# Low parts of h on VectorE with four buffers, the down product four units behind, stores on GpSimd's queue

## What is computed

```python
x = x + tanh(g_xattn[0]) * xattn(layernorm(x), ctx, Wq, bq, Wk, bk, Wv, bv, Wo, bo)   # 16 heads of 8
x = x + tanh(g_ffn[0])   * ffn(layernorm(x), ...)

# ffn, on x of (1792 tokens, 128)
logits  = x @ router_w.T + expert_bias                   # 160 experts
top_w, top_idx = top_k(sigmoid(logits), 8)
top_w   = top_w / (sum(top_w) + 1e-9) * 2.5
combine = zeros(T, 160); combine[t, top_idx] = top_w
h1w     = silu(einsum('th,eih->eti', x, w_gate)) * combine.T[:, :, None]     # 64 wide
routed  = einsum('eti,ehi->th', h1w, w_down)
shared  = silu(x @ w_gate_shared.T) @ w_down_shared.T
```

## Time and profile before

| | us |
|---|---|
| median of 3 runs | 1157.08 |
| lowest, highest | 1156.97, 1157.84 |
| the profiled execution | 1156.67 |
| its span, first to last instruction | 1155.1 |
| mean granted TensorE clock, as a share of full speed | 0.979 |

### The profile page before, as it was taken

The page is one execution under the profiler, slowest core; times in us unless marked ns, Lnnn a source line. Parts: engine busy times, 40 slices in busy tenths (PEclk is TensorE's granted clock), DMA queues, the critical chain, the costliest instruction groups (busy, mean ns, idle before and its releaser), DMA issues.

```text
span 1155.1 us, 37333 instructions
## 1 busy us (share of the span) xinstructions
PE 1072.5 (93%) x12102; PEld 708.9 (61%) x12102; DVE 965.2 (84%) x1695; ACT 845.5 (73%) x1810; POOL 613.2 (53%) x991
## 2 busy tenths in 40 slices
PE   3699899999999999999999998875999999999998
PEld 1376677777777777777777776522455555555554
DVE  4778688888888888888888888464999999999998
ACT  3476677777777777777777776544788888888887
POOL 6796987887888788788788884343000000000000
PEclk9899999999999999999999999978999999999999
DMA  7876867576675775767657523342588878877784
GB/s 158 158 177 164 171 171 170 129 195 154 150 182 134 177 168 147 173 146 176 169 131 192 126 79 77 116 129 74 200 224 239 231 228 229 234 228 239 223 231 124
DMA packets 229436, 197.10 MB, mean 171 GB/s; under 512 B 160687, under 2 KB 207343, under 8 KB 229398
## 3 DMA queue, kind: packets, MB, share of 16 engines
q1 hardware_dynamic: 218468, 174.14, 59.2%
q0 software_dynamic: 8960, 20.99, 6.4%
q10 hardware_dynamic: 1970, 1.49, 0.6%
HBM read 109.96 MB, written 12.55 MB: 106 GB/s over the span
## 4 chain that ended last, share of the span: by engine, by line
PE 73%; DVE 11%; issue 5%; SPq 4%; POOL 3%; DMA 3%; ACT 1%; DVEq 0%; POOLq 0%
PE bank L1500 15%; PE bank L1490 15%; PE bank L1301 11%; PE bank L1334 10%; PE bank L1315 10%; DVE part_max L968 6%; PE bank L1370 4%; PE bank L1358 4%; DVE rec L1106 3%; POOL ctT L672 1%; PE bank L1413 1%; SPq L412 1%; SPq L367 1%; DMA ctx_in<-in_ctx_dram 1%; SPq L359 1%
## 5 line engine op out<-in xcount | busy, mean ns | idle before, releaser
L761 ACT ACTIVATE p_exp<-bank 125x448 f32<-125x448 f32 x768 | 400.4, 544 | 193.1 <-PE bank L1315 192.0
L968 DVE TENSOR_REDUCE part_max<-bank 128x1 f32<-128x500 f32 x672 | 420.4, 670 | 70.0 <-PE bank L1334 69.2
L1315 PE MATMUL bank<-q_st,k_stk 97*125 97x224 f16 x1536 | 274.9, 263 | 10.0 <-DMA q_st<-neg_row 6.6
L1334 PE MATMUL bank<-kparts,q_blk 128*128 128x500 f16 x672 | 255.1, 383 | 15.8 <-DVE part_max L968 13.1
L1315 PEld LDWEIGHTS bank<-q_st,k_stk 97*125 97x125 f16 x1536 | 197.2, 138 | 74.2 <-ACT p_exp L761 12.7
L825 ACT ACTIVATE ctT<-bank 128x448 f32<-128x448 f32 x320 | 173.9, 544 | 57.0 <-PE bank L1490 24.0
L1500 PE MATMUL bank<-ctT,w_ring 128*128 128x448 f16 x864 | 210.6, 352 | 0.1
L831 ACT ACTIVATE ctT<-xnT 128x448 f16<-128x448 f32 x320 | 182.1, 569 | 20.2 <-DVE xnT L1157 17.7
L1301 PE MATMUL bank<-p_exp,v_sb 125*25 125x168 f32 (+1 forms) x6144 | 186.7, 262 | 2.3 <-DVE o_raw L982 2.3
L1166 DVE TENSOR_TENSOR ctT<-xnT,ctT 128x448 f16<-128x448 f32 (+1 forms) x297 | 183.7, 619 | 0.1
L1301 PEld LDWEIGHTS bank<-p_exp,v_sb 125*25 125x25 f32 x6144 | 142.5, 104 | 44.6 <-issue 2.5
(11 more groups left out here) (178 smaller groups left out, 1371.9 us busy)
## 6 DMA issues: line engine op xcount, KB each, us to landing
k_stk<-kparts SPq DMA_DIRECT2D x384, 93.8 KB, 3.3
v_sb<-c_scratch SPq DMA_DIRECT2D x72, 448.0 KB, 4.3
k_stk<-c_scratch SPq DMA_DIRECT2D x72, 448.0 KB, 4.3
ctx_in<-in_ctx_dram SPq DMA_DIRECT2D x30, 672.0 KB
w_scratch<-w_out POOLq DMA_DIRECT2D x80, 128.0 KB, 3.1
w_in<-in_L_ffn_w_gate_dram POOLq DMA_DIRECT2D x80, 64.0 KB, 3.3
w_in<-in_L_ffn_w_down_dram POOLq DMA_DIRECT2D x80, 64.0 KB, 3.4
ctx_in<-in_ctx_dram SPq DMA_DIRECT2D x30, 78.0 KB
```

Of the source, the lines that this page charges most:

```text
L761: act.activation(p_exp[0:KP, j % PR, f * 448:(f + 1) * 448], ST[f][0:KP, 0:448], ACT.Exp).then_inc(exp_done, 1)
L968: v.reduce_max(part_max[:, i // NCH, i % NCH:i % NCH + 1], SM[i % NSM][:, 0:CK], axis=AX.X).then_inc(sm_maxed, 1)
L1315: last = pe.matmul(ST[f][0:KP, (g % 2) * GC:(g % 2 + 1) * GC], k_stk[0:97, u, g, j * KP:(j + 1) * KP], q_st[0:97, u, g, :, :].rearrange("p ...
L1334: pe.matmul(SM[i % NSM][:, 0:CK], rows, kparts[:, u, 0, c * CK:(c + 1) * CK], start=True, stop=True).then_inc(sm_done, 1)
```

## The change

- The ahead stage's low parts move from POOL to DVE: `lo_part(k-1)` is issued behind `weigh(k)`; those of units 0 to 2 stand ahead of unit 3. POOL's loop L667 to L672 is gone.
- h has four places in this stage too. `h_f` moves from `xnT` to a part of `v_sb`. PE does down of unit k-4 ahead of up of unit k; only downs 0 and 1 stand ahead of unit 6.
- The four stores of combine weights are issued by POOL, behind its last `comb` operation; SP only waits for `c_stored[t]`.
- `c_first[t]` becomes two semaphores, one for each pair of DMAs, and DVE waits for the half that it reads next. The last tile is loaded by eight DMAs, two for each two experts, with one semaphore for each two.
- `late_scale` (four scalings) moves from DVE to ACT, as do the copy of the last tile's tokens into `xnT` and the two copies of its combine weights (`last_weights`). DVE gets one small operation, `late_shift`.
- `sums` goes ahead of `replaced` and has three instructions instead of four.
- Slots: the top 8 of tiles 1 and 2 one slot and one slot later, the transposes of the combine weights three slots earlier; in the ahead stage late rows after unit 3 (was 5), tokens at 10 (12), logits at 13 (15), sigmoid at 17 (18), top 8 at 18 (19), last transposes at 25 (24).

```diff
-    TOP_AT = {(B + 1, 1): 0, (B + 1, 2): 1, (B + 1, 3): 2}
-    COMBT_AT = {(B + 1, 8): 0, (B + 1, 11): 1, (B + 2, 2): 2}
+    TOP_AT = {(B + 1, 1): 0, (B + 1, 3): 1, (B + 1, 4): 2}
+    COMBT_AT = {(B + 1, 5): 0, (B + 1, 8): 1, (B + 1, 11): 2}
-    OUT_LATE, TOKENS_LATE, LOGITS_LATE, COMBT_LATE = 5, 12, 15, 24
+    ROWS_LATE, SCALE_LATE, TOKENS_LATE, LOGITS_LATE, PROB_LATE, TOP_LATE, COMBT_LATE = 3, 8, 10, 13, 17, 18, 25
...
-        h_f = xnT[:, :].rearrange("p (a t) -> p a t", a=NTC)
+        h_f = v_words[:, 2 * N:3 * N].rearrange("p (a t) -> p a t", a=NTC)
...
             for t in range(TS):
-                store(t)
+                sp.wait_ge(c_stored[t], 16)
                 for j in range(2):
                     for a in range(2):
...
-                        sp.dma_start(c_pairs[j][a::2, t, :, :], src).then_inc(c_first[t], 16)
+                        sp.dma_start(c_pairs[j][a::2, t, :, :], src).then_inc(c_first[t][j], 16)
...
-            store(TS)
+            sp.wait_ge(c_stored[TS], 16)
             sp.wait_ge(pv_done, B * KT)
-            for a in range(2):
-                src = c_scratch[0:AHEAD, a, TS * TC:N].unsqueeze(0).to_broadcast([I, AHEAD, TC])
-                sp.dma_start(c_last[a::2, :, :], src).then_inc(c_late, 16)
+            for j in range(AHEAD // 2):
+                for a in range(2):
+                    src = c_scratch[2 * j:2 * j + 2, a, TS * TC:N].unsqueeze(0).to_broadcast([I, 2, TC])
+                    sp.dma_start(c_last[a::2, 2 * j:2 * j + 2, :], src).then_inc(c_late[j], 16)
...
-            for k in range(TAIL):
-                b = k % TS
-                rows = slice(0, I if k < TS else 128)
-                pool.wait_ge(hh_done, k + 1)
-                until(pool, dn_done, earlier(k))
-                pool.tensor_tensor(h_lo[rows, b, :], h_f[rows, b, :], h_hi[rows, b, :], ALU.subtract).then_inc(hl_done, 1)
+            for c in range(NTC):
+                pool.wait_ge(cb_cp, 2 * c + 2)
+                pool.dma_start(c_scratch[:, :, c * TC:(c + 1) * TC], combT[0:EP, :, c * TC:(c + 1) * TC]).then_inc(c_stored[c], 16)
...
+            def late_scale():
+                act.wait_ge(shift_made, 1)
+                for p in range(*LATE):
+                    i = p - LATE[0]
+                    last = act.activation(xc[:, p, :], xt[:, p, :], ACT.Identity, scale=lst[:, 1, i:i + 1], bias=lst[:, 2, i:i + 1])
+                last.then_inc(xn_made, 1)
+            def last_weights(c):
+                for a in range(2):
+                    act.wait_ge(cb_tr, 2 * c + a + 1)
+                    act.activation(combT[0:EP, a, c * TC:(c + 1) * TC], CTB[2 * c + a][0:EP, 0:TC], ACT.Copy).then_inc(cb_cp, 1)
...
-                weigh(k, place(k), weighed(k), c_last[:, k - TAIL - 1, :])
-                lo_part(k - 1, place(k - 1), I if k - 1 == TAIL else 128)
+                m = k - TAIL - 1
+                if m % 2 == 0:
+                    dve.wait_ge(c_late[m // 2], 32)
+                weigh(k, k % NTC, weighed(k), c_last[:, m, :])
+                lo_part(k - 1, (k - 1) % NTC, I if k - 1 == TAIL else 128)
...
+            for k in range(TS - 1):
+                down_ahead(k)
+            for k in range(2 * TS, TAIL):
+                down_ahead(k - NTC)
+                up(k, z_place(k), (k - TS) % TS, w_ahead[(k - TS) // TS])
+                if k == TOKENS_LATE:
+                    tokens(TS)
+                if k == LOGITS_LATE:
+                    logits((4, 5))
+                if k == COMBT_LATE:
+                    weights_out(TS)
```

More of the change, by code:

```diff
@@ L819, in _, with silu, hi_part, shared @@
             attention(act, body, B, first=1)
-            def silu(k, b, r):
+            def silu(k, z, r):
                 act.wait_ge(z_done, k + 1)
                 until(act, h_done, r - 2)
-                act.activation(s_act[:, (b if isinstance(r, int) is False else r - 1) % 2, :], ZB[b][:, 0:TC], ACT.Silu)\
+                act.activation(s_act[:, (r - 1) % 2 if isinstance(r, int) else z % 2, :], ZB[z][:, 0:TC], ACT.Silu)\
                    .then_inc(s_done, 1)
-            def hi_part(k, b, r, downs=0):
+            def hi_part(k, b, r):
                 act.wait_ge(h_done, r)
-                until(act, dn_done, downs)
+                if isinstance(k, int):
+                    until(act, dn_done, h_free(k))
                 act.activation(h_hi[:, b, :], h_f[:, b, :], ACT.Copy).then_inc(hh_done, 1)
-            def shared(k, b):
+            def shared(k):
+                b = k % NTC
                 act.wait_ge(z_done, k + 1)
-                if k == TAIL:
-                    act.wait_ge(hl_done, earlier(k))
+                until(act, hl_done, h_free(k))
+                until(act, dn_done, h_free(k))
                 act.activation(h_f[0:I, b, :], ZB[b][0:I, 0:TC], ACT.Silu).then_inc(s_done, 1)
@@ L1486, in up @@
             def up(k, z, t, w):
[L1488 removed]
+                pe.wait_ge(s_done, z_free(k) if isinstance(k, int) else k - (NTC - 1))
                 for j, (a, b) in enumerate(hilo):
```

149 lines of the change are left out of this document (73 added, 76 removed).

## The result

The changed kernel takes 1143.1 us (median of four, 1141.91 to 1144.04), against 1157.03 us before on the same chip: a ratio of 0.9878, 95% interval 0.9861 to 0.9895. The gain is 14 us where 18.4 were forecast. The time lies inside the range, 4.4 us above the forecast. The profiled execution took 1142.26 us, its span is 1140.7.

What follows compares the result with a forecast made beforehand. The ahead stage was taken as bound by a 5.2 us chain per three units through POOL's low parts. Weigh of unit 28 moves from 809.3 to 790.9: 1156.67 - 18.4 = 1138.3, plus 0.4 to the median, 1138.7 us; range 1135 to 1146.

Steps and rivals of the forecast that it cites:

- end of the attention: Last attention steps: new slots put the o_raw copy ahead of the top 8 of tile 1, gaining 2.0 us (1.0 to 3.0).
- A: Stretch from the last attention steps' first keep-warm matmul to the shared expert's first up product; 2.0 us gain forecast.
- B: Stretch from the shared expert's first up product to weigh of unit 3: product -0.9 us, three low parts on DVE +1.65.
- C: Stretch from weigh of unit 3 to weigh of unit 26 in the ahead stage; forecast 39.4 us.
- Loads of tiles 1 and 2: First expert units: DVE's load waits go to nothing; SP issues twelve loads from 731.5 to 739.5, the last landing at 743.
- Ring of the ahead stage: Four places and down k-4 give a 3.5 us chain for four units, so a unit costs PE's 1.13 or DVE's work.
- rivals 1 and 3: PE's clock falls early, 1142 us, chance 0.17; or stays low through the whole ahead stage, 1156 us, chance 0.03.
- rival 2: Ahead stage: no side work hides, insertions add in full, 44.3 us instead of 39.4; time 1143.7 us, chance 0.11.
- Thirds: Ahead stage summed in three parts: units 3 to 8 10.1 us, 9 to 17 12.5, 18 to 25 16.8.
- Last tile: Combine weights before unit 28: copies end at 783.4, POOL store 3.3 us, first load of two experts 4.2.
- D: Stretch from weigh of unit 26 (forecast at 781.2) to weigh of unit 28 (forecast at 790.9).
- Rival 4: POOL's stores wait for descriptors while DVE is busy; slower than before from 17 us a store, 1161 at 18; chance 0.03.

Runs made afterwards that it cites:

- before_again: The kernel before, unedited, measured and profiled once more; 1156.99 us.
- after_again: The changed kernel, unedited, measured again on another chip; 1139.75 us, ratio 0.9824 to the kernel before.
- old_slots: Changed kernel with the attention's old slots for top 8 and combine-weight transposes; 1141.76 us, ratio 0.9856 to the kernel before.
- ring_alone: Changed kernel with POOL's low parts, SP's stores, last-tile loads in one piece and old attention slots back; 1149.58 us, ratio 0.9926 to the kernel before.
- three_behind: Changed kernel with down of unit k-3, not k-4, ahead of up of unit k, four places kept; 1146.93 us, ratio 0.9900 to the kernel before.
- late_whole: Changed kernel with the last tile's combine weights loaded by two DMAs with one wait; 1143.31 us, ratio 0.9866 to the kernel before.
- dense: Changed kernel with the last tile's top-8 work in one piece behind unit 18, transposes, copies and store four units earlier; 1133.48 us, ratio 0.9781.
- pool_low: Changed kernel with low parts on POOL again, four places kept; 1142.61 us, ratio 0.9855 to the kernel before.
- dense_early: As dense, with everything from the sigmoid on two slots earlier; 1135.22 us, ratio 0.9782 to the kernel before.
- dense_warm: dense_early plus 13 unused matmuls beside the last attention steps; 1133.54 us, ratio 0.9785 to the kernel before.
- sp_stores: Changed kernel with the four stores issued and awaited on SP again; 1141.09 us, ratio 0.9829 to the kernel before.
- warm: Changed kernel plus 13 unused matmuls beside the last attention steps; 1140.12 us, ratio 0.9837 to the kernel before.

## Why the prediction was right, and where it missed

**The marks, one by one.** Weigh of unit 3: 741.8 forecast, 746.23 found. From there to weigh of unit 28: 49.1 forecast, 48.70 found. So the ring and everything behind it, where 17 of the 18.4 us were, came out within 0.4 us, and the miss lies ahead of unit 3. (The profiled execution lies 0.84 us below its median, before's 0.41: the other 0.4.) There it has two terms. 2.1 us lie ahead of anything that the change touches: the keep-warm matmuls begin at 711.89 instead of 709.76. This is no property of the two kernels, for in before_again they begin at 712.07; what makes it isn't shown (the start alone doesn't, see after_again). The prediction carried before's absolute times over without a word on how far they repeat. The other 2.4 us are the step *end of the attention*: A should have become 25.9 (27.92 - 2.0) and was 28.33. B fits: 6.01, where 5.29 - 0.9 + 1.65 gives 6.04. (The prediction's own sum for unit 3 gives 741.72, which it wrote as 741.8.)

Luck has a part in how near the number came. The forecast takes before's marks from one profile. From the marks of before_again, weigh of unit 3 at 746.09 and of unit 28 at 810.05, the same steps give unit 28 at 793.9 and a time of 1140.9 us, 2.2 below the measured 1143.1; and against before_again C falls by 13.7 us, not 16.3. What doesn't hang on this is the length of the changed stage, 49.1 forecast and 48.70 and 49.48 found in the two profiles of the changed kernel.

**End of the attention, the step that failed.** The wait for o_raw is gone, as forecast, but for a cause that the prediction didn't name. It gave it to the new slots. With the old slots (old_slots, ring_alone) the wait is gone too, and DVE is the one that waits for PE there, 0.2 us. What went is read from the timelines, and it is in `sums`; no run takes back `sums` alone. Timeline of before, DVE and POOL:

```profile
715.42 1.52 DVE L1063 TENSOR_SCALAR wsum<-wsum 112x4 f32<-112x4 f32 x1
...
719.56 1.51 DVE L1063 TENSOR_SCALAR wsum<-wsum 112x4 f32<-112x4 f32 x1
```
```profile
715.38 1.53 POOL L663 TENSOR_TENSOR ctx_in<-kparts,ctx_in 112x640 f32<-112x640 f32 x1 [13.07 <-DVE ctx_in L1057]
```

The operation on 112x4 elements starts 0.04 us behind POOL's and ends with it, at 716.9. In the new order `sums` stands ahead of `replaced`, so for tile 0 POOL hasn't started yet, and the operation of the same kind and size in after takes 0.17:

```profile
716.52 0.17 DVE L1086 TENSOR_SCALAR wsum<-wsum 112x4 f32<-112x4 f32 x1
```

That is 1.35 us on DVE and, from one MAX8 group to the next, 4.15 us in before and 2.72 in ring_alone (718.43 - 715.71). Two tiles of it are 2.9 us, more than the wait of 2.35. A second row, of tile 1 in ring_alone, shows that it is POOL's operation that holds DVE's: POOL's started at 718.60 and took 1.54, to 720.14, and DVE's, started at 719.68, ended with it after 0.49.

```profile
719.68 0.49 DVE L1092 TENSOR_SCALAR wsum<-wsum 112x4 f32<-112x4 f32 x1
```
```profile
718.60 1.54 POOL L669 TENSOR_TENSOR ctx_in<-kparts,ctx_in 112x640 f32<-112x640 f32 x1 [13.73 <-DVE ctx_in L1085]
```

The Trainium skill, SBUF — State Buffer, section "SBUF: two separate sides", calls the port pair that VectorE and GpSimd share an exclusive lock that the first holds for its whole instruction; the rows of before and of ring_alone agree. The prediction had quoted that page for the store and read it off, and didn't look for it in `sums`.

What ate this gain in after is TensorE's clock. A is 25.05 in three kernels whose code up to there is that of after (three_behind, late_whole, dense), -2.9 us against before, within the 1 to 3 of the prediction. In after and five others the clock fell in 716 to 728 us, and A was 26.8 to 28.4. Timelines of PE, first after, then late_whole, 0.94 us earlier throughout:

```profile
711.89 2.46 PE L1445 MATMUL bank<-q_hi,sg 128*64 128x448 f16 x12
...
717.13 0.84 PE L1339 MATMUL bank<-q_st,k_stk 97*125 97x224 f16 x4 [1.35 <-ACT p_exp L760]
718.26 0.98 PE L1339 MATMUL bank<-q_st,k_stk 97*125 97x224 f16 x4 [0.29 <-ACT p_exp L760]
719.16 1.71 PE L1325 MATMUL bank<-p_exp,v_sb 125*25 125x168 f32 x32
```
```profile
710.95 2.46 PE L1444 MATMUL bank<-q_hi,sg 128*64 128x448 f16 x12
...
716.19 0.84 PE L1338 MATMUL bank<-q_st,k_stk 97*125 97x224 f16 x4 [1.35 <-ACT p_exp L759]
717.32 0.75 PE L1338 MATMUL bank<-q_st,k_stk 97*125 97x224 f16 x4 [0.29 <-ACT p_exp L759]
718.00 0.97 PE L1324 MATMUL bank<-p_exp,v_sb 125*25 125x168 f32 x32
```

The two are the same in every row from 696 us on, durations and waits to 0.01 us, up to the second score group of those shown; then one goes on at the lower level (2.4 to 1.2 GHz, 0.97 becomes 1.71) and the other doesn't. The prediction had put the slow 32 matmuls of the earlier trace rows down to the wait for o_raw ahead of them, and counted them as gone with it. In before_again the clock had fallen ahead of that wait (716 to 722 us: 0.76, against 0.99 in before). So the fall belongs to neither kernel and its cause stays open, and a gain that rests on a clock that stays up should have been given a chance, not counted.

**Loads of tiles 1 and 2.** No wait, as forecast, but SP issued the last two loads at 742.10 to 744.7 and not by 739.5: store 2, issued behind the loads of tiles 0 and 1 at 736.84, took 5.26 us from its issue to that of its load and not 3.1. The prediction's last sign of being wrong was a wait of SP for a store above 5 us; SP itself waited 3.9 of these 5.26, so the sign was nearly met, and the price that the prediction gave for it, 1 to 2 us for a store 3 us longer, wasn't paid. It was enough, since unit 5 came at 750.54. In an execution whose clock stayed up the load has the same lead: in late_whole store 2 is issued at 732.61, its load at 738.15, and unit 3 comes at 742.01. With SP's stores and the old slots, in ring_alone, unit 5 waited 4.42 us.

**Ring of the ahead stage.** Right: four units in a ring that is shorter than their work. three_behind puts 6.1 us on the distance of four with DVE's low parts, and pool_low 1.7 on the engine once that is there. The fourth place without the longer distance is what three_behind has; the distance of four without the fourth place wasn't run. Where the work is the bound the sums held: the clock was 1.00 from 746 to the sigmoid, so rivals 1 and 3 didn't happen; C is 39.52 and not 44.3, so rival 2 didn't.

**Thirds.** 11.1 us for units 3 to 8 (forecast 10.1): behind ScalarE's four scalings, 1.65 us in all and priced at 1.6, DVE stood idle 1.13 us, and 0.42 ahead of unit 5, where 0.6 had been put. Units 9 to 17, without the 2.99 us in which DVE waits for the sigmoid's table loads: 12.7 (12.5). Units 18 to 25 with them: 15.8 (16.8), eight units of 1.07 on DVE, 4.2 us of side work and those 2.99. The clock's fall behind the sigmoid came (0.58 in 776 to 780) but lay beside DVE's work, busy 3.93 of these 4 us, and the 1.0 us put down for it wasn't needed. The 39.52 beside 39.4 is thus partly two misses that cancel.

**Last tile.** Copies ended 1.3 us behind weigh of unit 26 instead of 2.2, store 3.57 (3.3), first load 4.03 (4.2): D 9.18 instead of 9.7. DVE's wait for that load was 6.77 us, where 5 to 6 had been given. late_whole confirms the price of the pieces. Rival 4 and the rule that the prediction took from the Trainium skill, SBUF — State Buffer, section "SBUF: two separate sides" (a DMA from GpSimd starved by a busy VectorE) asked for a POOL store beside weighs and low parts. In after there was none: behind low part 26 at 787.53 DVE has nothing to do up to unit 28, and the prediction had taken it for busy. dense has one, from 778.66 to 781.49 with DVE busy 2.10 of 2.83 us, and dense_early and dense_warm repeat it (2.83 and 2.84 us, DVE busy 2.21 and 2.28). That is less than the 3.34 to 4.03 us of the seven profiles with a POOL store beside a nearly idle DVE. So a busy DVE didn't hold these stores up; the operations that the rule's sentence names, copies in SBUF, weren't among DVE's, and of those no run shows anything. What the prediction left as PE idle for 4 us was the largest sum still to be had: dense takes 4.5 to 5.3 us out of it.

The gap has a second price, which lies behind unit 28, in the stretch that the prediction took for the same in both kernels. In after and before the clock falls when PE takes up its work there; in dense it doesn't. Windows of after and of dense, both 2 to 6 us behind weigh of unit 28:

```profile
796.93:800.93 4.00, 4.00 (x15) 1.70 (x15) 2.45 (x5) 1.88 (x5) 0.00 (x0) 0.64 0.87 238
```
```profile
789.87:793.87 4.00, 4.00 (x23) 2.08 (x23) 3.94 (x8) 3.41 (x7) 0.00 (x0) 1.00 0.91 322
```

From weigh of unit 28 to the end it is 343.7 to 344.6 us in the seven profiles whose clock stays up there, 345.5 to 346.2 in the five in which it falls, and 346.8 and 347.1 in late_whole and ring_alone, which have the longest D (12.48 and 11.85) and the longest fall. The three kernels without the gap are all among the seven; but so are pool_low, old_slots, sp_stores and warm, which have it, so closing the gap isn't the only way to be spared.

## What to carry to other kernels

When an engine waits in every turn of a ring, count how many turns it spans before moving its work: one more unit between up and down, which needs one more place, was worth 6.1 us here with the low part on the faster engine, and moving the low part there 1.7 with the longer ring in it. When a small operation takes nine times its usual time, look at what GpSimd does at that moment; moving it by one position in the order is free. And when a stretch of side work ends in a round trip through DRAM, do it in one piece as early as its inputs allow, even if the units beside it stop for a while.

## What the runs showed of the hardware

- The first weights arrived between 10.9 and 14.0 us in fourteen profiles with the same code at the start. A point 700 us further on, by the same code, was reached between 708.4 and 712.7 us, and not in the order of the starts.
- With the same instructions, durations and waits ahead of it, TensorE's clock fell in one execution at 718.3 us and stayed up in another; a fall there cost 2.3 to 3.3 us (A with the same slots). Behind the gap of the last tile a fall went with some 2 us more up to the end (345.5 to 346.2 against 343.7 to 344.6).
- A 112x4 operation of VectorE took 1.51 us when a GpSimd operation on 112x640 had just started, 0.49 when it came in later, and 0.17 without it; a product of 112x640 on DVE 0.82 us instead of 1.68.
- A store of 280 KB by GpSimd, from its issue to that of the load behind it, took 2.8 us beside a VectorE busy for three quarters of it, in three profiles, and 3.3 to 4.0 beside a nearly idle one, in seven. Issued among the broadcast loads of other tiles it took 5.3 us from GpSimd's queue in after and 5.5 in late_whole and dense, and from SP's 3.7 to 6.4 us (3.92 in before_again and 6.35 in before for the same store).
